# The layer-norm offset added on TensorE in the last stage, instead of on GpSimd in an earlier one

## The reference

```
def _layernorm(x, g, b):
    return (x - mean(x)) * rsqrt(var(x) + EPS) * g + b        # over the 512 features
x = _layernorm(x + _L0_gnn_ref(...))                           # 1250 x 512: "x_rows"
for l in range(2):                                             # in _L1_gnn_ref, from x
    attention over edges (8 heads), output product, batch norm, feed-forward, batch norm
x = _layernorm(x + _L1_gnn_ref(x, ...))                        # _L1 ends in its own layer norm with ln_g, ln_b
```

## Time and profile before

| | us |
|---|---|
| median of 3 executions | 1952.17 |
| the three | 1944.32, 1952.17, 1953.27 |
| the profiled execution, its own time | 1944.32 |
| its span, first to last instruction | 1942.2 |
| lying around the span | 2.1 |
| first `stage_attend` (about 1015 to 1322) | 307 |
| second `stage_attend` (about 1504 to 1811) | 307 |
| `stage_final` (from about 1893) | 49 |

### The profile page before, as it was taken

One profiled execution on the slowest core, in us unless ns is written; L12 is line 12 of the kernel. 1 busy time (PEld: TensorE's weight loads), 2 busy tenths in 40 slices (PEclk: granted clock), 3 DMA queues, 4 the chain that ended last, 5 costly groups with the idle time before them and its releaser, 6 DMA issues. The chain is left out here.

```text
span 1942.2 us, 35951 instructions
## 1 busy us (share of the span) xinstructions
PE 1668.4 (86%) x14216; PEld 1543.0 (79%) x14216; DVE 1303.4 (67%) x2316; ACT 1115.7 (57%) x1682; POOL 121.8 (6%) x106
## 2 busy tenths in 40 slices
PE   5997799997586999991988999998688899999861
PEld 5896799997465999991877888888688788888861
DVE  5884899993337999956426766675642567676567
ACT  2454688885214888873436777773343577767430
POOL 0000000000450000002001000000200100000020
PEclk7998899999796999995998999999889899999985
DMA  4111122211313110001675333102057533310203
GB/s 159 45 45 43 68 95 98 94 55 47 110 37 120 44 40 38 26 1 64 164 195 136 90 69 75 37 2 54 8 163 202 135 85 73 71 43 1 55 1 111
DMA packets 82455, 145.61 MB, mean 75 GB/s; under 512 B 13302, under 2 KB 52318, under 8 KB 81038
## 3 DMA queue, kind: packets, MB, share of 16 engines
q1 hardware_dynamic: 82318, 143.73, 25.9%
HBM read 95.21 MB, written 37.13 MB: 68 GB/s over the span
## 5 line engine op out<-in xcount | busy, mean ns | idle before, releaser
L1119 PE MATMUL banks<-h_gat,probs_t_gat 125*125 (+2 forms) x3200 | 373.8, 273 | 0.0
L1119 PEld LDWEIGHTS banks<-h_gat,probs_t_gat 125*125 125x125 f32 x3200 | 364.6, 190 | 0.0
L1619 ACT COPY probs_t_att<-banks 125x1250 f32<-125x1250 f32 x160 | 192.3, 1202 | 172.9 <-PE banks L1578 172.9
L1074 DVE SCALAR_TENSOR_TENSOR probs_gat<-a_src_pair_gat,a_dst_gap_gat,a_low_pair_gat 125x1250 f32<-125x1250 f32 x160 | 240.2, 1502 | 24.3 <-DMA a_low_pair_gat<-a_src_rows 24.3
L1646 DVE CUSTOM_DVE_ANT_0 probs_att<-banks,logs_or_y 125x1250 f32<-125x1250 f32 x160 | 233.5, 1459 | 30.3 <-PE banks L1569 30.3
L1111 PE MATMUL banks<-ident,probs_gat 125*125 125x125 f32 x1600 | 211.1, 280 | 49.4 <-ACT probs_gat L1041 49.4
L1079 DVE CUSTOM_DVE_ANT_0 probs_gat<-probs_gat,log_counts 125x1250 f32<-125x1250 f32 x160 | 233.4, 1459 | 0.0
L1111 PEld LDWEIGHTS banks<-ident,probs_gat 125*125 125x125 f32 x1600 | 192.9, 193 | 50.8 <-ACT probs_gat L1041 50.8
L1041 ACT ACTIVATE probs_gat<-probs_gat,neg_max_gat 125x1250 f32<-125x1250 f32 x160 | 212.7, 1330 | 33.5 <-DVE neg_max_gat L1079 33.0
L1612 ACT ACTIVATE probs_att<-probs_att,neg_max_att 125x1250 f32<-125x1250 f32 x160 | 214.9, 1343 | 11.0 <-DVE neg_max_att L1646 10.9
L1590 PE MATMUL banks<-probs_t_att,v_rows 125*64 125x125 f32 x3200 | 206.5, 275 | 0.1
(11 more groups left out here) (210 smaller groups left out, 2619.4 us busy)
## 6 DMA issues: line engine op xcount, KB each, us to landing
logs_or_y<-log_rows SPq DMA_DIRECT2D x20, 610.4 KB
q_first<-q_rows SPq DMA_DIRECT2D x12, 1000.0 KB, 17.0
q_rows<-q_out_qkv SPq DMA_DIRECT2D x40, 250.0 KB
a_src_pair_gat<-a_src_rows SPq DMA_DIRECT2D x16, 610.4 KB
a_low_pair_gat<-a_src_rows SPq DMA_DIRECT2D x16, 610.4 KB
q_att<-q_rows SPq DMA_DIRECT2D x8, 1000.0 KB, 17.5
log_counts<-counts_fr SPq DMA_DIRECT2D x50, 122.1 KB
gat_rows<-final_gat SPq DMA_DIRECT2D x16, 312.5 KB
```

The lines of the kernel that those rows point to most:

```text
L1074: dve.scalar_tensor_tensor(probs[:, n.tile % B], a_src[:, n.parity], a_dst_gap[:, n.tile, bass.ds(n.head, 1)], a_low[:, n.parity], ALU.add ...
L1119: total = pe.matmul(out_bank(n.tile), probs_t[:, n.tile % B, i], h_sb[:, i, bass.ds(n.head * CH, CH)], start=i == 0, stop=i == T - 1)
L1619: act.copy(probs_t[:, u % TURNED].rearrange("p (b c) n -> p b (c n)", c=2), turned).then_inc(probs_saved, 1)
```

## The change

Nothing is added to x in `stage_attend` any more: GpSimd's additions, the loads of ln_b and of the pairs, the stores, their semaphores and the array `x_biased` go. In `stage_final` x comes from `x_rows`, ln_b is loaded as one row of 512 to one partition, and VectorE sets a row of 125 ones. For each tile TensorE then makes x + ln_b in a PSUM bank with two float32 matmuls of 512 columns, one with the identity as weights and x as the moving operand, one of the ones row with ln_b. VectorE's add reads that bank (`x_bank`) instead of `x1`. The 8 banks are divided: 4 for the turned features, 4 for x, RING becomes 4.

```diff
-def stage_attend(k, ..., rows, att, x_rows, ln_b, x_biased):
+def stage_attend(k, ..., rows, att):
...
-                load_x(r)
...
-        @block.gpsimd
-        def _(pool):
-            pool.wait_ge(bias_loaded, 16)
-            for r in range(T // 2):
-                pool.wait_ge(x_loaded, 16 * (r + 1))
-                for i in range(2):
-                    done = pool.tensor_tensor(x_pair[:, i], x_pair[:, i], bias_rows[:], ALU.add)
-                done.then_inc(x_added, 1)
...
-def stage_final(k, cols, ln_g, x_biased, out):
+def stage_final(k, cols, ln_g, ln_b, x_rows, out):
...
-    RING = 8
+    RING = 4
...
+        def x_bank(t):
+            return k.psum[0:P, (RING + t % RING) * BANK:(RING + t % RING + 1) * BANK]
...
             sp.dma_start(g[:], ln_g.rearrange("(o d) -> o d", o=1).to_broadcast([P, D])).then_inc(g_loaded, 16)
+            sp.dma_start(b[:], ln_b.rearrange("(o d) -> o d", o=1)).then_inc(b_loaded, 16)
...
+            def bias(t):
+                if t % 2 == 0:
+                    pe.wait_ge(x1_loaded[t // 2], 16)
+                if t == 0:
+                    pe.wait_ge(b_loaded, 16)
+                    pe.wait_ge(ones_set, 1)
+                if t >= RING:
+                    pe.wait_ge(added, t - RING + 1)
+                pe.matmul(x_bank(t), k.ident[0:P, 0:P], x1[:, t], start=True, stop=False)
+                pe.matmul(x_bank(t), ones_row[:], b[:], start=False, stop=True).then_inc(biased, 1)
+
+            for t in range(RING):
+                turn(t)
             for t in range(T):
-                turn(t)
+                bias(t)
+                if t + RING < T:
+                    turn(t + RING)
...
                     dve.wait_ge(gained, t + 1)
-                    if t % 2 == 0:
-                        dve.wait_ge(x1_loaded[i], 16)
-                    dve.scalar_tensor_tensor(z[:, t], z[:, t], inverse[:, 0, t:t + 1], x1[:, t], ALU.mult, ALU.add
+                    dve.wait_ge(biased, t + 1)
+                    dve.scalar_tensor_tensor(z[:, t], z[:, t], inverse[:, 0, t:t + 1], x_bank(t), ALU.mult, ALU.add
                                              ).then_inc(added, 1)
...
+            dve.memset(ones_row[:], 1.0).then_inc(ones_set, 1)
             measure_first(0)
```

More of the change, by code:

```diff
@@ L1463, in _, with stage_attend @@
             run_steps(dve, CHUNKS, 1, step)
-def stage_attend(k, q_rows, q_first, k_halves, v_rows, logs, log_rows, rows, att, x_rows, ln_b, x_biased):
+def stage_attend(k, q_rows, q_first, k_halves, v_rows, logs, log_rows, rows, att):
     nc, P, T, N, D, H = k.nc, k.P, k.T, k.N, k.D, k.H
@@ L1485, in stage_attend @@
         neg_max, sums, sums_safe, inverse = (sb(what, [P, COLUMNS]) for what in ("neg_max", "sums", "sums_safe", "inverse"))
-        x_pair, bias_rows = sb("x_pair", [P, 2, D]), sb("bias_rows", [P, D])
-        x_loaded, x_added, x_stored = (k.sem(f"{what}_att") for what in ("x_loaded", "x_added", "x_stored"))
-        bias_loaded = k.sem("bias_loaded_att")
         q_loaded = [k.sem(f"q_loaded{i}_att") for i in range(2)]
@@ L1520, in load_logs @@
                 sp.dma_start(logs[:, t % KEPT], log_rows[t * P:(t + 1) * P, :]).then_inc(logs_loaded[t % KEPT], 16)
[L1522 to L1531, removed]
             for r in range(T // 2):
@@ L1535, in _ @@
                     load_q(r)
-                if r == 0:
-                    sp.dma_start(bias_rows[:], ln_b.rearrange("(o d) -> o d", o=1).to_broadcast([P, D])).then_inc(bias_loaded, 16)
-                load_x(r)
                 if r == 1:
@@ L1931, in stage_final @@
         z, x1 = sb("z", [P, T, D]), sb("x1", [P, T, D])
-        g = sb("g", [P, D])
+        g, b, ones_row = sb("g", [P, D]), sb("b", [1, D]), sb("ones_row", [1, P])
         stats, moments = sb("stats", [P, 2, T, 6]), sb("moments", [P, 2, T, 2])
         spread, deviation, inverse = (sb(what, [P, 2, T]) for what in ("spread", "deviation", "inverse"))
-        g_loaded, turned, gained, added, stats_done, moments_done, out_stored = (
-            k.sem(f"{what}_fin") for what in ("g_loaded", "turned", "gained", "added", "stats_done", "moments_done",
-                                              "out_stored"))
+        g_loaded, b_loaded, ones_set, turned, gained, biased, added, stats_done, moments_done, \
+            out_stored = (
+                k.sem(f"{what}_fin") for what in ("g_loaded", "b_loaded", "ones_set", "turned", "gained", "biased",
+                                                  "added", "stats_done", "moments_done", "out_stored"))
         spread_done, deviation_done, inverse_done = ([k.sem(f"{what}{r}_fin") for r in range(2)]
@@ L1955, in load @@
             def load(i):
-                sp.dma_start(x1[:, 2 * i:2 * i + 2], x_biased.rearrange("(t p) d -> p t d", p=P)[:, 2 * i:2 * i + 2]
+                sp.dma_start(x1[:, 2 * i:2 * i + 2], x_rows.rearrange("(t p) d -> p t d", p=P)[:, 2 * i:2 * i + 2]
                              ).then_inc(x1_loaded[i], 16)
@@ L2074, in build @@
         x_cols = k.dram("x_cols", [D, N])
-        x_biased = k.dram("x_biased", [N, D])
         with ExitStack() as gat_ctx:
@@ L2133, in build @@
             rows = weight_rows(k, ctx, "rest", (Wo, W1, W2))
-            stage_attend(k, q_rows, q_first, k_halves, v_rows, logs, log_rows, rows, feature_cols, x_rows,
-                         a["L1_gnn_ln_b"], x_biased)
+            stage_attend(k, q_rows, q_first, k_halves, v_rows, logs, log_rows, rows, feature_cols)
             stage_tail(k, feature_cols, x_cols, rows, w["bo"][layer], w["b1"][layer], w["b2"][layer],
                        ((w["g1"][layer], w["beta1"][layer]), (w["g2"][layer], w["beta2"][layer])), y, feature_cols)
-        stage_final(k, feature_cols, a["L1_gnn_ln_g"], x_biased, a["out"])
+        stage_final(k, feature_cols, a["L1_gnn_ln_g"], a["L1_gnn_ln_b"], x_rows, a["out"])
 INPUTS = ("x", "src", "dst") + tuple(f"L0_gnn_{name}" for name in (
```

2 lines of the change are left out of this document (removed).

## The result

| | before | after |
|---|---|---|
| median, us | 1946.37 (1940.92 to 1953.27, 6 runs) | 1957.94 (1956.51 to 1959.99, 6 runs) |
| ratio of the two | | 1.006, 95% interval 1.0042 to 1.0078 |
| profiled execution, its own time | 1944.32 | 1963.22 |
| its span | 1942.2 | 1961.4 |

The changed kernel is slower by 11.6 us, interval 8 to 15. The predicted 1958.3 lies 0.4 us from the measured median, but that is luck, two errors that cancel: the forecast stood on a median of 1952.2 for the kernel before, which six runs put at 1946.4, and it added 6.1 us where 11.6 were measured. No measurable change, the likeliest outcome by the forecast, was not what happened. In size, though not in its cause, the result is nearest case B, +12.

A forecast was written before the change was run, and what follows sets the result against it. VectorE was taken to bound the last stage, TensorE the attend stages. Losses of 4.4 + 4.0 = 8.4 us less 2.3 give +6.1, on 1952.2 that is 1958.3 us; range 1947.5 to 1968.5.

The forecast's parts named there:

- No measurable change: Whole kernel: result within about 0.5%, 9.8 us, of the kernel before; chance 0.65.
- case B: Last stage: clock stays at 0.50 because TensorE works in bursts with idle time between; +12 us in all, 1964; chance 0.22.
- What bounds the kernel: TensorE sets the pace in the attend stages, VectorE in the last; each wait put into VectorE's order there delays the end equally.
- The attend stages, 2.3 us: Both attend stages: without GpSimd's additions multiplications by the inverse sum shorten, giving back 2.3 us, bounds 0 and 6.3; fewer DMAs give 0.
- VectorE's add from PSUM, 0: Last stage: VectorE's add reading a PSUM bank instead of SBUF costs 0, within 0.2 us for all ten.
- The price of a product at full clock, 0.88 us: Last stage: one float32 product of 512 columns on TensorE at clock 1.00 takes 0.88 us, lower end 0.47.
- At the low clock, 1.76: Last stage: at clock 0.50 a product's price doubles to 1.76 us, a tile's pair to 3.52.
- The order, odd tiles behind transposes: Last stage: products of tiles 1, 3, 5 stand behind transposes waiting for VectorE, so they are exposed; even tiles' products come hidden.
- tiles 7 and 9: Last stage: no transposes stand ahead of their products, so these are hidden behind VectorE's work.
- group 0: Last stage, tiles 0 and 1: VectorE's second add 4.4 us late; 2.1 at full clock throughout, 6.1 at half.
- groups 1 and 2: Last stage: loss of 0.9 us at clock 1.00 or 3.15 at 0.50 each; taken as 2.0 us each, 4.0 together.
- groups 3 and 4: Last stage: products run ahead, so loss 0; up to 2 us at half clock throughout.

The follow-up runs named there:

- the order run: Changed kernel with both products of a pair of tiles issued ahead of the transposes that wait for VectorE; 1.0035 of before, 1949.6 us, last stage 48.4 us.

## Why the prediction was right or wrong

**What bounds the kernel:** right for the kernel before. The last stage was VectorE's, and every wait put into its order there came out at the end: 18.1 us of waits, 18.8 us of stage. For the changed kernel it was wrong: there TensorE bounds the stage. The prediction set the total of the products aside ("Not the total counts") because 18 us at full clock are less than VectorE's 33. At the clock that was granted, products and transposes are 45.3 us, and the total does count.

**The attend stages, 2.3 us:** right, shown by two traces with the additions and twelve without: 1 to 3. The 20 DMAs and the 153.5 us of queue waits gave nothing, as argued.

**VectorE's add from PSUM, 0:** right; one add is 0.74 to 0.75 us, as before.

**The price of a product at full clock, 0.88 us:** right, 0.86 where one on 125 rows follows another. In "FP8 and Floating Point Precision", section TensorE Precision Notes, the Trainium skill has true FP32 take 4 passes; from that 512 columns are an estimated 0.85 us at 2.4 GHz and 1.71 at 1.2. The traces agree, with 0.86 and 1.70. **At the low clock, 1.76:** the changed kernel pays 2.0. When 125 rows and one row alternate, the weight load is not hidden: 1.70 against 2.0 at 0.50, 0.86 against 1.05 at 1.00 (in the order run). In the timeline above the load of the ones row begins with its own product, at 1904.87; where products on 125 rows follow each other, at 0.50, it begins a record earlier (1916.90 for a record at 1917.75, in the run with all rows).

**The order, odd tiles behind transposes:** it is where the waits show, but by itself it cost little, the 2.5 us in which TensorE stood idle. The run that changed it brought 11.6 us back, most of them through the clock. And tiles 7 and 9, which I had called hidden at full clock, were not: a pair took 4.0 us, and so VectorE waited in six adds. Against the terms of the sum: group 0, 2.9 and 4.1 us for tiles 0 and 1, in all 7.0 where 4.4 stood; groups 1 and 2, 3.8 each where 2.0 stood; groups 3 and 4, 1.6 and 2.0 where 0 stood.

**The step that failed** is in group 0: "By then TensorE has worked for over 4 us and I take the clock as 1.00 for tile 1", and with it the mixed 2.0 us for groups 1 and 2. The clock stayed at 0.50 from the first product to the last. The 1.00 was read off a rise that transposes of 128 rows had made, as if time at work were all that counts. The run with all rows for ln_b shows that it is not: with the second product on 125 rows instead of one, the clock was 1.00 some 3 us after the first product. The two runs with one kind of product say the same: on 125 rows it rose with TensorE busy 6.2 of 11 us, on one row never, with 11.0 of 11. Half of the changed kernel's product time is on one row. Case B had the clock right and the size nearly (+14.4 in the stage, measured 18.8, with pairs of 4.0 us instead of 3.5), but its cause, idle time between bursts, was not there: TensorE was hardly idle.

In "TensorE: Matmul & The Clock Gate", section PE-mode transpose, the Trainium skill says that the full clock does not engage for transposes. The traces do not agree: in all fourteen the clock rose to 1.00 some 2.9 to 3.6 us after the stage's first transpose, with nothing but transposes on TensorE. The prediction was right to leave that rule out of its sum.

**What is not settled.** The median grew by 11.6 us (8 to 15), the traced stage by 18.8, less 2.3 in the attend stages. In the six other runs with an interval that same sum of the trace lies inside it; in the changed kernel, 16.5, it lies just outside. In 24 executions of the changed kernel the time goes with the mean granted clock, from 1953.5 us at 0.924 to 1965.2 at 0.915; the traced one, 1963.2 at 0.917, is among the slow of them. But the kernel before does the same, 1931.4 us at 0.929 and 1949.3 at 0.917 beside the experiments, so that this need not come from the last stage. The traces show another place: what lies ahead of the first attend stage, the same code in all, takes 1011.9 us in the fastest of the fourteen and 1022.9 in the slowest. One trace a kernel cannot say more about the median. The executions of before beside the experiments have medians of 1940.9, 1942.0 and 1943.1, and the 24 of the changed kernel 1959.0; the 16 to 18 us between them would fit the trace, but they were not taken side by side.

Nor is it shown why the clock behaves so. The order run has the same mix of one-row and full-row products and a clock that rises at times; what tips it was not isolated.

## What to carry to other kernels

An engine that is idle on average is not a free place for work: ask what stands ahead of the new work in its queue, when its inputs land, and at which clock it will run. Then add up all the work of both engines at the lower clock too: here that alone says that TensorE would be the slower one. A bias added by a product of a ones row with one row of data looks like the cheapest of products, but it cost as much as one on 125 rows; next to those its weight load was in the open, and with it the clock stayed low. If such work must go to TensorE, start it before anyone waits, put it in one burst ahead of instructions that wait for others, and give it all rows.

## What the runs showed of the hardware

The granted clock does not follow the busy share alone: with one-row products TensorE was busy 11.00 of 11.00 us at 0.50, with full-row ones busy 6.20 of 11.00 us at 0.66.

A float32 product of 512 columns is two records, 0.86 us on 125 rows at 1.00 and 1.70 at 0.50. One-row products behind each other take 1.7 at 0.50 as well. Where the two kinds alternate, each takes 0.19 us more at 1.00 and 0.3 at 0.50.

In the attend stages multiplications of 0.87 us took up to 1.94 us beside GpSimd's additions, and none was over 0.88 without them. A GpSimd addition beside VectorE can hold up even an operation on two columns; one of them, in the run with GpSimd in the last stage, took 1.26 us instead of 0.17:

```profile
1901.13 2.48 POOL L1945 TENSOR_TENSOR x_fin<-x_fin,ln_b_rows 125x512 f32<-125x512 f32 x2 [4.54 <-DMA x_fin<-x_rows]
1901.15 1.26 DVE L1981 TENSOR_SCALAR spread_fin<-moments_fin 125x2 f32<-125x2 f32 x1
```
